# Attention and FP4 feed-forward block on one core: reciprocals as exp(-ln) on ScalarE, another order of loads and of the whole program, and 20 pairs of unread products

## The chip, the cores and the metric

The kernel runs on one NeuronCore of a Trainium2 chip. Its engines are TensorE (PE, matrix products into the PSUM banks), VectorE (DVE), ScalarE (ACT), GpSimdE (POOL) and SyncE (SP, which here only issues transfers). Each engine runs its own queue in order and waits on semaphores. The metric is the device time of one execution in microseconds, and the median of several executions is compared.

## The reference, cut to what matters

```python
x = L0_attn_x                                   # (8, 512, 128), float32
xn = (x - mean) / sqrt(var + 1e-5)
# attention branch, 16 heads of 8, two codes per head
q, k, v = heads(xn @ w_qkv.T)
q = q @ code.T * 8**-0.5;  k = k @ code.T * 8**-0.5      # two codes per head
q = softmax(q, axis=-1) * 8**-0.5
k_exp = exp(k - max(k, axis=rows))
kv = cumsum(k_exp * v, axis=rows) / (cumsum(k_exp, axis=rows) + 1e-9)
attn = sum(q * kv, over codes) @ w_out.T
# feed-forward branch, everything through block-wise FP4 (blocks of 16)
gate = fp4(xn) @ fp4(w_gate).T;  up = fp4(xn) @ fp4(w_up).T     # 352 wide
ffn = fp4(silu(gate) * up) @ fp4(w_down).T
out = x + attn + ffn
```

`fp4` divides a block of 16 by its largest magnitude over 6, rounds to the grid 0, 0.5, 1, 1.5, 2, 3, 4, 6 and multiplies back. The two denominators that matter for the change are the variance under the square root and, for every row, head and code, the product of the softmax sum of q and the running sum of k_exp.

## The kernel before, in words

The eight batches are the unit of the pipeline. One batch is a tile of 128 partitions by 512 elements (four rows of 128 on each partition). The program of each engine is a loop over steps with the pieces of work of several batches in it. Which batch a piece works on follows from `b = step - k`, and the order in which the pieces stand in the loop body is written out by hand (it differs on each engine). A piece that belongs to the weights or to the first batches stands under `if step == k`. So each engine has a fill (the weights are made FP4, the first batches enter), a part in which every step repeats the same pieces for other batches, and a drain.

In the repeated part one turn of TensorE is, by the names of the destinations: `t_ps` from `wv_t` (the values), `o_ps` (output rows), `t_ps` from `xq` (transposes), `h_ps` (transposes of the hidden blocks), `o_ps`, then the gate and up products `g_ps`, `u_ps`, the coded q and k products `a_ps` from `wqk_t` (called qk below), `t_ps` from `o_codes`, and so on to `a_ps` from `kv` and `before` (called the base product below: the column sums over the preceding rows).

The step that the change rewrites is the chain from the base product to `q_n`:

- ACT: `a_ps<-q_rel` (exp of the q codes), after the semaphore `base_done`
- DVE: `kv<-kv,a_ps` adds the base to the running sums (128x1152), `a_ps<-a_ps` adds the two exps, `den` multiplies both sums, in two instructions
- DVE: `den_r` is the reciprocal of `den`, and `q_n` is the exp times `den_r`
- POOL: `o_codes` is `kv` times `q_n`. TensorE waits for `qn_done` before the qk products of a later batch, since they write the same PSUM bank `a_ps`.

Beside it ACT brings `xq_t` from PSUM (TensorE waits for it before the gate product), makes the square `s_ps<-yx` of the rounding of x (DVE turns it into `sx` and `qx`) and the silus. Exp and Silu sit in different function tables, so ACT loads a table twice in a turn, and once more for the Sqrt of the variances of batches 2 to 7 (`sd`, line 551).

At the start TensorE multiplies `ident` by `before` 14 times (line 905) into `o_ps`, whose content nobody reads.

## Time and profile before

| | us |
|---|---|
| median of 3 executions | 153.87 (152.71 to 154.32) |
| the profiled execution | 152.51 |
| its span, first to last instruction | 150.8 |
| outside the span | 1.7 |
| first gate product of batch 0, 1, 2, 3 | 25.7, 40.2, 54.3, 68.7 |
| first gate product of batch 7 | 124.5 |

The profile is one execution. Its busy shares are means over a fill (to about 40 us), a repeated part (54.3 to 111.7 us, four turns of 14.33 us) and a drain (from 124.5 us), which have different limits. Each stretch is therefore read by itself. PE is TensorE's products, PEld its weight loads. "x2" behind a product of float32 numbers counts two records for one product.

### The profile page before, as it was taken

The numbers are of one execution on the slowest core, as the hardware profiler recorded it, in microseconds if no ns is written. First come the engines' busy times: TensorE is split into PE (matmuls) and PEld (weight loads), VectorE is DVE, ScalarE is ACT, GpSimd is POOL, SyncE is SP. The second block draws the span as 40 slices with busy tenths as digits, with TensorE's granted clock in tenths as the row PEclk, the third lists the DMA queues.
The fourth block names the chain that finished last, engine by engine and source line by source line (L and its number), as shares of the span: only waits on it lengthen the run. The fifth ranks groups of instructions, "written<-read, shape, count | busy, mean of one in ns | idle before, by whom it ended". The sixth has DMA issues, their size and how long they took to land.

```text
span 150.8 us, 2457 instructions
## 1 busy us (share of the span) xinstructions
PE 131.9 (87%) x817; PEld 106.2 (70%) x817; DVE 127.6 (85%) x326; ACT 111.4 (74%) x252; POOL 120.1 (80%) x123
## 2 busy tenths in 40 slices
PE   3937694998699999999999999999999999985591
PEld 3926373565476978797879778987988797675490
DVE  0699997169999999999999999999999989999601
ACT  0547549379889889988998899889894978592430
POOL 4418756616999999999999999999999999966710
PEclk9997555599999999999999999999999999999998
DMA  5980000000000001000100010001000100200101
GB/s 123 309 335 5 0 0 0 7 0 0 2 0 0 0 4 70 0 2 0 70 4 0 0 70 7 0 0 70 0 4 21 48 0 0 76 0 0 70 0 70
DMA packets 3932, 5.15 MB, mean 34 GB/s; under 512 B 528, under 2 KB 1872, under 8 KB 3920
## 3 DMA queue, kind: packets, MB, share of 16 engines
q1 hardware_dynamic: 2832, 4.36, 8.3%
q10 hardware_dynamic: 1088, 0.64, 1.5%
q8 instruction: 6, 0.10, 0.3%
q14 instruction: 6, 0.05, 0.1%
HBM read 2.90 MB, written 2.10 MB: 33 GB/s over the span
## 4 chain that ended last, share of the span: by engine, by line
PE 69%; DVE 11%; ACT 8%; DMA 4%; POOL 3%; ACTq 2%; issue 1%
PE t_ps L1040 5%; PE a_ps L928 4%; DMA x_all<-x 4%; PE g_ps L1073 4%; PE u_ps L1077 3%; PE u_ps L1074 3%; PE o_ps L1047 3%; PE o_ps L1012 3%; PE g_ps L911 3%; PE g_ps L935 3%; PE g_ps L974 3%; PE u_ps L953 3%; PE o_ps L918 3%; PE o_ps L1068 3%; PE t_ps L1003 3%; PE u_ps L984 2%
## 5 line engine op out<-in xcount | busy, mean ns | idle before, releaser
L349 POOL TENSOR_TENSOR kv<-v_sb,kv 128x512 f32<-128x512 f32 x16 | 16.9, 1075 | 0.0
L385 POOL TENSOR_TENSOR o_codes<-kv,q_n 128x1024 f32<-128x1024 f32 x8 | 15.8, 1972 | 1.4 <-DVE q_n L766 1.4
L438 POOL TENSOR_TENSOR yh<-h,h_r 128x704 f32<-128x704 f32 x8 | 11.1, 1385 | 5.7 <-ACT h_r L464 5.7
L608 ACT ACTIVATE xn<-x_all,shift,rstd 128x128 f32<-128x128 f32 x32 | 13.1, 481 | 1.4 <-POOL shift L433 1.4
L371 POOL TENSOR_TENSOR yh<-h,h_r 128x704 f32<-128x704 f32 x8 | 11.1, 1385 | 1.4 <-ACT h_r L557 1.4
L323 POOL TENSOR_TENSOR hq<-qh,h_max 128x704 f32<-128x704 bf16 x8 | 11.1, 1385 | 0.9 <-DVE qh L862 0.9
L342 POOL TENSOR_TENSOR yx<-xn,x_r 128x512 f32<-128x512 f32 x8 | 8.5, 1058 | 4.0 <-ACT x_r L504 4.0
L1040 PE MATMUL t_ps<-wv_t,xn_t 128*128 128x128 f32 x64 | 9.7, 299 | 2.1 <-ACT xn_t L494 1.9
L401 POOL TENSOR_TENSOR hq<-qh,h_max 128x704 f32<-128x704 bf16 x8 | 11.1, 1387 | 0.0
L1040 PEld LDWEIGHTS t_ps<-wv_t,xn_t 128*128 128x128 f32 x64 | 8.6, 208 | 3.2 <-ACT xn_t L494 3.2
L712 DVE TENSOR_TENSOR kv<-kv,a_ps 128x1152 f32<-128x1152 f32 x8 | 10.7, 1333 | 0.0
L569 ACT ACT_TABLE_LOAD x8 | 10.3, 1283 | 0.1
L928 PEld LDWEIGHTS a_ps<-wqk_t,xn_t 128*128 128x128 f32 x64 | 8.9, 211 | 1.8 <-ACT wqk_t L516 1.2
L928 PE MATMUL a_ps<-wqk_t,xn_t 128*128 128x64 f32 x64 | 9.0, 288 | 1.0 <-ACT wqk_t L516 1.0
L800 DVE TENSOR_TENSOR out_sb<-x_all,o_ps 128x512 f32<-128x512 f32 x8 | 5.4, 678 | 5.2 <-PE o_ps L918 5.2
L946 PE MATMUL t_ps<-ident,o_codes 128*128 128x128 f32 x32 | 7.5, 276 | 2.6 <-POOL o_codes L385 2.5
L477 ACT ACT_TABLE_LOAD x7 | 9.0, 1283 | 0.1
L334 POOL TENSOR_TENSOR xq<-qx,x_max 128x512 f32<-128x512 bf16 x8 | 8.5, 1057 | 0.6 <-DVE qx L751 0.6
L1073 PE MATMUL g_ps<-wg_t,xq_t 128*128 128x352 f32 x16 | 6.9, 519 | 2.2 <-ACT xq_t L562 2.2
L591 ACT ACTIVATE silu<-g_ps 128x352 f32<-128x352 f32 x8 | 3.7, 463 | 6.0 <-PE g_ps L911 6.0
L758 DVE RECIPROCAL den_r<-den 128x128 f32<-128x128 f32 x8 | 7.6, 944 | 0.1
L533 ACT ACTIVATE v_sb<-t_ps 128x512 f32<-128x512 f32 x8 | 4.8, 596 | 3.7 <-PE t_ps L1040 3.7
(195 smaller groups left out, 466.7 us busy)
## 6 DMA issues: line engine op xcount, KB each, us to landing
out<-out_sb SPq DMA_DIRECT2D x8, 256.0 KB, 2.0
x_all<-x SPq DMA_DIRECT2D x7, 256.0 KB, 6.2
x_all<-x ACTq DMA_DIRECT2D x1, 256.0 KB, 5.8
w_raw<-w_down SPq DMA_DIRECT2D x1, 176.0 KB, 4.5
wqk_raw<-w_qkv ACTq DMA_DIRECT2D x1, 128.0 KB, 3.5
w_raw<-w_gate SPq DMA_DIRECT2D x1, 128.0 KB, 3.1
w_raw<-w_up ACTq DMA_DIRECT2D x1, 128.0 KB, 3.9
wv_t<-w_qkv ACTq DMA_DIRECT2D x1, 64.0 KB, 5.5
```

Of the source, the lines that this page charges most:

```text
L323: nc.gpsimd.tensor_tensor(hq[:, 4 * p + 2:4 * p + 4, 0:FF].rearrange("p t (b k) -> p t b k", k=BLOCK), qh[:, p, 2 * FF:4 * FF].rearrange(" ...
L349: last = nc.gpsimd.tensor_tensor(heads(kv[:, p, :, c * D:(c + 1) * D]), heads(v_sb[:, p, :].rearrange("p (j d) -> p j d", j=TILES)), widen ...
L371: nc.gpsimd.tensor_tensor(blocks(yh[:, p, 2 * FF:4 * FF], PAIR * HB), h[:, p, 2 * HB:4 * HB, 0:BLOCK], spread(h_r[:, p, 2 * HB:4 * HB], PA ...
L385: nc.gpsimd.tensor_tensor(o_codes[:, p, :, :].rearrange("p j (c w) -> p j c w", w=HEAD), kv[:, p, :, 0:KV].rearrange("p j (c w) -> p j c w ...
L401: nc.gpsimd.tensor_tensor(hq[:, 4 * p + 0:4 * p + 2, 0:FF].rearrange("p t (b k) -> p t b k", k=BLOCK), qh[:, p, 0 * FF:2 * FF].rearrange(" ...
L438: nc.gpsimd.tensor_tensor(blocks(yh[:, p, 0 * FF:2 * FF], PAIR * HB), h[:, p, 0 * HB:2 * HB, 0:BLOCK], spread(h_r[:, p, 0 * HB:2 * HB], PA ...
L569: nc.scalar.activation(silu[:, 1, :], g_ps[:, 0:FF], ACT.Silu).then_inc(silu1_done, 1)
L608: last = nc.scalar.activation(xn[:, p, j * D:(j + 1) * D], x_all[:, b, j * D:(j + 1) * D], ACT.Identity, bias=shift[:, b, j:j + 1], scale= ...
L712: nc.vector.tensor_tensor(kv[:, p, :, :], kv[:, p, :, :], a_ps[:, 0:ROW].unsqueeze(1).broadcast_to([P, TILES, ROW]), ALU.add)
L928: last = nc.tensor.matmul(a_ps[:, 2 * j * HC:2 * (j + 1) * HC], xn_t[:, p, j * P:(j + 1) * P], wqk_t[:, :], start=(j == 0), stop=False, sk ...
L1040: last = nc.tensor.matmul(t_ps[:, j * P:(j + 1) * P], xn_t[:, p, j * P:(j + 1) * P], wv_t[:, :], start=True, stop=True)
L1073: nc.tensor.matmul(g_ps[:, 0:FF], xq_t[:, p, 1 * P:2 * P], wg_t[:, :], start=True, stop=True).then_inc(gate1_done, 1)
```

## The change

It rewrites three things and moves nearly all the rest.

1. `den_r` is no longer DVE's reciprocal. ACT computes `den_log = ln(den)` and `den_0 = exp(-den_log)`; DVE computes `den_p = den * den_0` and `den_r = (den_p - 2) * den_0`, which is a Newton step with the sign turned, and `q_n` takes the scale `-HEAD_SCALE`. The square root of the variances of batches 2 to 7 becomes `ln` and `exp(-0.5 * ...)` in the same way, in two groups (batches 2 and 3, batches 4 to 7). One table holds Exp and Ln, and is loaded by name.
2. The third piece of `w_up` goes to SP's queue, `w_down` to ACT's, and batch 1 of x to SP's.
3. Instead of 14 unread products there are 20 pairs, spread over the fill.

```diff
-            sp.dma_start(w_raw[:, 2 * FFP:], w_down).then_inc(down_in, 16)
-            for b in range(2, BATCHES):
+            sp.dma_start(w_raw[0:FF - 2 * P, FFP + 2 * P:2 * FFP], w_up[2 * P:FF, :]).then_inc(gu_in, 16)
+            for b in range(1, BATCHES):
...
-            act.dma_start(w_raw[0:FF - 2 * P, FFP + 2 * P:2 * FFP], w_up[2 * P:FF, :]).then_inc(gu_in, 16)
             act.dma_start(wv_t[:, :], w_qkv[2 * D:3 * D, :]).then_inc(wv_in, 16)
-            act.dma_start(x_all[:, 1, :], x_v[1]).then_inc(x_in[1], 16)
+            act.dma_start(w_raw[:, 2 * FFP:], w_down).then_inc(down_in, 16)
+            nc.scalar.preload_act_table_set(LOG_SET)
...
-                if step == 5:
-                    act.wait_ge(vareps2_done, 1)
-                    nc.scalar.activation(sd[:, 2:8, :], var_eps[:, 2:8, :], ACT.Sqrt).then_inc(sd2_done, 1)
+                if step == 6:
+                    act.wait_ge(vareps2_done, 1)
+                    nc.scalar.activation(var_log[:, 2:4, :], var_eps[:, 2:4, :], ACT.Ln).then_inc(vlog2_done, 1)
...
+                    act.wait_ge(den_done, b + 1)
+                    nc.scalar.activation(den_log[:, :, :], den[:, :, :], ACT.Ln).then_inc(dlog_done, 1)
...
+                    nc.scalar.activation(den_0[:, :, :], den_log[:, :, :], ACT.Exp, scale=-1.0).then_inc(dexp_done, 1)
...
+                    nc.vector.tensor_tensor(den_p[:, :, :], den[:, :, :], den_0[:, :, :], ALU.mult).then_inc(dprod_done, 1)
...
+                    nc.vector.scalar_tensor_tensor(out=den_r[:, :, :], in0=den_p[:, :, :], scalar=2.0, in1=den_0[:, :, :], op0=ALU.subtract, op1=ALU.mult).then_inc(denr_done, 1)
...
-                    nc.vector.reciprocal(den_r[:, :, :], den[:, :, :]).then_inc(denr_done, 1)
...
-            for _ in range(14):
-                nc.tensor.matmul(o_ps[:, 0:P], ident[:, :], before[:, :], start=True, stop=True)
...
+                if step == 7:
+                    for _ in range(2):
+                        nc.tensor.matmul(o_ps[:, 0:P], ident[:, :], before[:, :], start=True, stop=True)
```

The order of the pieces shows in the queues. ACT in a turn of the repeated part, from the copy of `xn_t` to the first silu, before:

```order
L494 ACTIVATE xn_t<-t_ps 128x512 [waits xnT_done]
L504 ACTIVATE x_r<-x_recip 128x32 [waits xrec_done]
L524 ACTIVATE a_ps<-q_rel 128x128 [waits base_done]
L528 ACTIVATE hq_t<-h_ps 128x384 [waits hqT2_done]
L533 ACTIVATE v_sb<-t_ps 128x512 [waits v_done]
L543 ACTIVATE s_ps<-yx 128x512 [waits qh0_done,yx_done]
L557 ACTIVATE h_r<-h_recip 128x44
L562 ACTIVATE xq_t<-t_ps 128x512 [waits xqT_done]
L569 ACT_TABLE_LOAD
L569 ACTIVATE silu<-g_ps 128x352 [waits gate1_done]
```

The same place of ACT now:

```order
L484 ACTIVATE a_ps<-q_rel 128x128 [waits base_done]
L489 ACTIVATE x_r<-x_recip 128x32 [waits xrec_done]
L505 ACTIVATE h_r<-h_recip 128x44 [waits hrec1_done]
L516 ACTIVATE s_ps<-yh 128x352 [waits yh0_done]
L521 ACTIVATE v_sb<-t_ps 128x512 [waits v_done]
L534 ACTIVATE hq_t<-h_ps 128x384
L538 ACTIVATE den_log<-den 128x128 [waits den_done]
L551 ACTIVATE den_0<-den_log 128x128 [waits dlog_done]
L556 ACTIVATE xq_t<-t_ps 128x512 [waits xqT_done]
L563 ACTIVATE s_ps<-yx 128x512 [waits qh0_done,yx_done]
L567 ACT_TABLE_LOAD
L567 ACTIVATE silu<-g_ps 128x352 [waits gate1_done]
```

The copy `xq_t` now stands behind both new functions, which wait for DVE's `den`, and the square `s_ps<-yx` stands behind `xq_t` instead of ahead of it. DVE at the same place of a turn, before:

```order
L640 RECIPROCAL x_recip<-x_max 128x32 [waits xmax_done]
L645 SCALAR_TENSOR_TENSOR sh<-s_ps,yh 128x352 [waits sqh0_done]
L661 RECIPROCAL h_recip<-h_max 128x44 [waits hmax1_done]
L679 SCALAR_TENSOR_TENSOR qh<-s_ps,sh 128x352 [waits sh0_done]
L712 TENSOR_TENSOR kv<-kv,a_ps 128x1152 [waits qexp_done]
L713 TENSOR_REDUCE a_ps<-a_ps 128x64
L723 SCALAR_TENSOR_TENSOR sx<-s_ps,yx 128x512 [waits sqx_done]
L729 SCALAR_TENSOR_TENSOR den<-kv,a_ps 128x4x16 [waits qsum_done]
L729 SCALAR_TENSOR_TENSOR den<-kv,a_ps 128x4x16
L751 SCALAR_TENSOR_TENSOR qx<-s_ps,sx 128x512 [waits sx_done]
L758 RECIPROCAL den_r<-den 128x128 [waits den_done]
L766 SCALAR_TENSOR_TENSOR q_n<-a_ps,den_r 128x128 [waits denr_done]
```

And now:

```order
L691 RECIPROCAL h_recip<-h_max 128x44 [waits hmax1_done]
L693 TENSOR_REDUCE a_ps<-a_ps 128x64 [waits qexp_done]
L695 TENSOR_TENSOR kv<-kv,a_ps 128x1152
L698 SCALAR_TENSOR_TENSOR den<-kv,a_ps 128x4x16 [waits badd_done]
L698 SCALAR_TENSOR_TENSOR den<-kv,a_ps 128x4x16
L703 SCALAR_TENSOR_TENSOR sh<-s_ps,yh 128x352 [waits sqh0_done]
L716 SCALAR_TENSOR_TENSOR qh<-s_ps,sh 128x352 [waits sh0_done]
L725 TENSOR_TENSOR den_p<-den,den_0 128x128 [waits dexp_done]
L766 SCALAR_TENSOR_TENSOR den_r<-den_p,den_0 128x128 [waits dprod_done]
L784 SCALAR_TENSOR_TENSOR sx<-s_ps,yx 128x512 [waits sqx_done]
L789 SCALAR_TENSOR_TENSOR q_n<-a_ps,den_r 128x128 [waits denr_done]
L802 SCALAR_TENSOR_TENSOR qx<-s_ps,sx 128x512 [waits sx_done]
```

`q_n` now stands behind `sx`, which waits for ACT's late square. TensorE at the end of the same turn, the products from the first gate product on, before:

```order
L1073 MATMUL g_ps<-wg_t,xq_t 128x352 [waits xqt_done]
L1074 MATMUL u_ps0<-wu_t,xq_t 128x352
L1077 MATMUL u_ps1<-wu_t,xq_t 128x352
L911 MATMUL g_ps<-wg_t,xq_t 128x352 [waits silu1_done]
L916 MATMUL o_ps<-wo_t,o_t 128x128 [waits hqt3_done]
L918 MATMUL o_ps<-wd_t,hq_t 128x128 x3
L928 MATMUL a_ps<-wqk_t,xn_t 128x64 [waits qn_done]
```

And now:

```order
L998 MATMUL g_ps<-wg_t,xq_t 128x352 [waits xqt_done]
L1001 MATMUL u_ps1<-wu_t,xq_t 128x352
L1015 MATMUL a_ps<-wqk_t,xn_t 128x64 [waits qn_done]
L1015 MATMUL a_ps<-wqk_t,xn_t 128x64 x3
L1022 MATMUL g_ps<-wg_t,xq_t 128x352 [waits silu1_done]
L1029 MATMUL u_ps0<-wu_t,xq_t 128x352
```

The qk products with their wait for `q_n` now come two products behind the gate product, where six stood between. At last TensorE's first instructions in the fill; before, 14 unread products, the weight product of line 968 and then the transposes of batch 0. Now:

```order
L1070 MATMUL o_ps<-before,ident 128x128 x2
L1098 MATMUL a_ps<-code_bd,wqk_raw 128x32 [waits codebd_done]
L1098 MATMUL a_ps<-code_bd,wqk_raw 128x32
L1119 MATMUL o_ps<-before,ident 128x128 x2
L1086 MATMUL o_ps<-before,ident 128x128 x2
L1103 MATMUL o_ps<-before,ident 128x128 x2
L1116 MATMUL o_ps<-before,ident 128x128 x2
L1122 MATMUL o_ps<-before,ident 128x128 x2
L1145 MATMUL t_ps<-ident,xn 128x128 [waits xn_done]
```

Eight pairs stand ahead of the weight product (the last is the first row here) and five behind it. One pair follows these transposes, three stand behind the first qk products and ahead of the transpose of `k_max`, and three more come one by one in the first two turns.

## Rows read from the trace of the kernel before

**Rows 1.** The page: the span, the busy times and the chain that ended last.

```profile
span 150.8 us, 2457 instructions
PE 131.9 (87%) x817; PEld 106.2 (70%) x817; DVE 127.6 (85%) x326; ACT 111.4 (74%) x252; POOL 120.1 (80%) x123
...
PE 69%; DVE 11%; ACT 8%; DMA 4%; POOL 3%; ACTq 2%; issue 1%
```

**Rows 2.** Stretches: length, busy PE, PEld, DVE, ACT, POOL, granted clock, DMA.

```profile
8.55:13.30 4.75, 1.81 (x12) 1.38 (x12) 4.55 (x21) 2.35 (x9) 2.63 (x3) 1.00 0.49 187
13.30:30.20 16.90, 13.20 (x41) 9.43 (x42) 12.67 (x62) 10.45 (x25) 11.18 (x15) 0.50 0.01 2
30.20:40.17 9.97, 8.01 (x42) 5.07 (x40) 8.55 (x20) 8.16 (x21) 5.45 (x5) 0.99 0.00 0
...
54.32:68.65 14.33, 14.33 (x98) 11.95 (x98) 13.85 (x31) 13.01 (x30) 14.06 (x13) 1.00 0.05 19
```

**Rows 3.** The fill in order of time: start, length, engine.

```profile
2.44 5.33 PE L905 MATMUL o_ps<-before,ident 128*128 128x128 f32 x28 [2.44 <-POOL head_of L365]
...
10.35 0.24 ACT L456 ACTIVATE w_r<-w_recip 128x48 f32<-128x48 f32 x1 [1.86 <-DVE w_recip L803]
```

**Rows 4.** The chain that ended last, in the fill and at the first turns.

```profile
16.31 0.90 PE h_ps L939 x3
17.21 0.23 PE t_ps L980
...
23.67 1.28 ACT L551
...
25.73 1.54 PE g_ps L1073 x2
...
29.61 1.06 PE g_ps L911 x2
...
40.17 0.86 PE g_ps L1073 x2
```

**Rows 5.** One turn in order of time, from q_n on.

```profile
98.36 0.29 DVE L766 SCALAR_TENSOR_TENSOR q_n<-a_ps,den_r 128x128 f32<-128x128 f32 x1
...
100.31 0.97 PEld L928 LDWEIGHTS a_ps<-wqk_t,xn_t 128*128 128x128 f32 x8
...
107.90 0.28 ACT L524 ACTIVATE a_ps<-q_rel 128x128 f32<-128x128 f32 x1
...
108.61 1.33 DVE L712 TENSOR_TENSOR kv<-kv,a_ps 128x1152 f32<-128x1152 f32 x1
...
109.12 0.60 ACT L533 ACTIVATE v_sb<-t_ps 128x512 f32<-128x512 f32 x1 [0.40 <-PE t_ps L1040]
109.62 0.60 ACT L543 ACTIVATE s_ps<-yx 128x512 f32<-128x512 bf16 x1
...
109.87 0.28 DVE L713 TENSOR_REDUCE a_ps<-a_ps 128x64 f32<-128x128 f32 x1
...
110.25 0.69 DVE L723 SCALAR_TENSOR_TENSOR sx<-s_ps,yx 128x512 f32<-128x512 f32 x1
...
110.47 0.60 ACT L562 ACTIVATE xq_t<-t_ps 128x512 f32<-128x512 f32 x1
...
110.86 0.34 DVE L729 SCALAR_TENSOR_TENSOR den<-kv,a_ps 128x64 f32<-128x64 f32 x2
...
111.72 0.94 DVE L758 RECIPROCAL den_r<-den 128x128 f32<-128x128 f32 x1
```

**Rows 6.** The chain that ended last, in the same turn: TensorE's slots.

```profile
100.58 0.84 PE a_ps L928 x8
...
107.38 0.49 PE a_ps L1019 x2
...
111.65 0.59 PE g_ps L1073 x2
```

**Rows 7.** The chain that ended last, in the drain.

```profile
136.94 0.96 DVE den_r L758
```

More of the change, by code:

```diff
@@ new lines, in _ @@
+                    dve.wait_ge(badd_done, b + 1)
+                    for c in range(CODE):
+                        last = nc.vector.scalar_tensor_tensor(out=den[:, :, c * HEADS:(c + 1) * HEADS], in0=kv[:, p, :, KV + c * HEADS:KV + (c + 1) * HEADS],
+                                                              scalar=DEN_EPS, in1=a_ps[:, ROW + TILES * HC:ROW + TILES * (HC + HEADS)].rearrange("p (j h) -> p j h", j=TILES),
+                                                              op0=ALU.add, op1=ALU.mult)
@@ new lines, in _ @@
+                if step == 5:
+                    dve.wait_ge(wsq_u_done, 1)
+                    nc.vector.scalar_tensor_tensor(out=w_s[:, FFP:2 * FFP], in0=u_ps[0][:, 0:FFP], scalar=OFFSET, in1=w_y[:, FFP:2 * FFP],
+                                                   op0=ALU.add, op1=ALU.subtract)
+                if step == 6:
+                    dve.wait_ge(x_in[5], 16)
+                    for j in range(TILES):
+                        last = nc.vector.bn_stats(stats[:, 5, j, :], x_all[:, 5, j * D:(j + 1) * D])
@@ new lines, in _ @@
+                if step == 10:
+                    for c in range(CHUNKS):
+                        last = nc.tensor.transpose(h_ps[:, c * P:(c + 1) * P], w_dq[:, 2 * FFP + c * P:2 * FFP + (c + 1) * P], ident[:, :])
+                if step == 3:
+                    for _ in range(2):
+                        nc.tensor.matmul(o_ps[:, 0:P], ident[:, :], before[:, :], start=True, stop=True)
+                b = step - 9
+                if 0 <= b < BATCHES:
+                    p = b % 2
+                    if b < BATCHES - 1:
+                        pe.wait_ge(vev_done, b + 2)
+                    if b == 0:
+                        pe.wait_ge(xq_done, b + 1)
+                    for j in range(TILES):
+                        last = nc.tensor.transpose(t_ps[:, j * P:(j + 1) * P], xq[:, p, j * P:(j + 1) * P], ident[:, :])
+                    last.then_inc(xqT_done, 1)
@@ new lines, in _ @@
+                b = step - 11
+                if 0 <= b < BATCHES:
+                    p = b % 2
+                    pe.wait_ge(hqt2_done, b + 1)
+                    for c in range(CHUNKS):
+                        last = nc.tensor.transpose(h_ps[:, c * P:(c + 1) * P], hq[:, 4 * p + 3, c * P:(c + 1) * P], ident[:, :])
+                    last.then_inc(hqT3_done, 1)
+                    nc.tensor.matmul(o_ps[:, 2 * P:3 * P], o_t[:, p, 2 * P:3 * P], wo_t[:, :], start=True, stop=False)
+                    for c in range(CHUNKS):
+                        last = nc.tensor.matmul(o_ps[:, 2 * P:3 * P], hq_t[:, 2, c * P:(c + 1) * P], wd_t[:, c * P:(c + 1) * P], start=False, stop=(c == CHUNKS - 1))
@@ L908, in _ @@
+                b = step - 9
                 if 0 <= b < BATCHES:
@@ L911, in _ @@
                     nc.tensor.matmul(g_ps[:, 0:FF], xq_t[:, p, 0 * P:1 * P], wg_t[:, :], start=True, stop=True).then_inc(gate0_done, 1)
-                b = step - 6
+                if step == 3:
+                    for _ in range(2):
+                        nc.tensor.matmul(o_ps[:, 0:P], ident[:, :], before[:, :], start=True, stop=True)
+                b = step - 9
+                if 0 <= b < BATCHES:
+                    p = b % 2
+                    nc.tensor.matmul(u_ps[0][:, 0:FF], xq_t[:, p, 0 * P:1 * P], wu_t[:, :], start=True, stop=True).then_inc(up0_done, 1)
+                b = step - 11
                 if 0 <= b < BATCHES:
```

1021 lines of the change are left out of this document (539 added, 482 removed).

## The prediction

> **What bounds the kernel now.** I read the page first [rows 1]: TensorE is busy 87% of a span of 150.8 us and has 69% of the chain that ended last, but DVE, POOL and ACT have 85, 80 and 74%, so every engine is nearly full and the order of the queues decides. Then the table of stretches [rows 2], because the means hide three different limits. In the repeated part a turn is 14.33 us and TensorE is busy for all of it, at a granted clock of 1.00 (2.4 GHz). There nothing that DVE, ACT or POOL gains shortens the time; an added wait of TensorE lengthens it. DVE has 13.85 us of work in such a turn, ACT 13.01, POOL 14.06, so 0.5, 1.3 and 0.3 us are free. In the fill the clock is 0.50 (1.2 GHz) from 13.3 to 30.2 us; it fell after a stretch from 8.55 to 13.30 in which TensorE was busy 1.81 of 4.75 us, and rose after an unbroken row of products. The first gate product of batch 0 takes 1.54 us, that of batch 1 0.86 [rows 4]. So the fill is the place where time is to be had, and the repeated part the place where it can be lost five times over. The sum is made against the profiled execution, 152.51 us (span 150.8 and 1.7 around it); that is 1.4 below the median of 153.87, and I carry the difference over to the median.
>
> **The loads.** The third piece of w_up has the same place in time on SP's queue as it had on ACT's, ahead of w_down instead of beside it, and batch 1 of x is issued some 0.5 us earlier. The reciprocal that waits for the weights' maxima still comes behind both, and `w_r` starts at 10.35 [rows 3]. What could be earlier by the loads is at most the half microsecond of the issue; I take 0, range -0.5 to +0.3. What hides them is DVE, busy 4.55 of 4.75 us there [rows 2].
>
> **The fill up to the first gate product of batch 0.** First the unread products. Fourteen took 5.33 us, 0.38 each [rows 3]. Now 26 of the 40 stand ahead of the transposes of batch 0: from 2.44 sixteen end at 8.5, the weight product takes 0.5, ten more end at 12.9. `xn` of batch 0 now stands behind `w_r` on ACT, hence starts at 10.5 and ends at about 12.2, so the products cost it 0.7 us. Transposes, copy, a pair (0.8), the value products and the qk products bring TensorE to about 16.2, and three more pairs (2.3 us) to 18.5, where the transpose of `k_max` stood at 17.2 [rows 4]. That is **+1.3 us**. From there to the gate product it took 8.5 us. Of the nine pieces of TensorE on the chain from 16.31 to 29.61 (the first and the last are shown), three lie between that transpose and the gate product, 3.9 us together at half clock [rows 4]. Since TensorE is busy almost without a gap from 2.4 to 18.5 now, I take it that the clock stays at 2.4 GHz in what follows, and every piece falls by 40 to 50%, as the gate product's 1.54 to 0.86: about **-1.8 us** on the pieces up to the gate product. The table load for Sqrt, 1.28 us on the chain [rows 4], and the square root behind it go, since Ln and Exp share the resident table; four small functions for batches 2 and 3 come in their place, at some 0.1 each behind other work: **-1.2 us**. Sum -1.7: the first gate product at 24.0 instead of 25.7. Two things could keep it later: w_q of the up weights is now rounded behind `qx` and `k_max`, about 4 us later, and the copy of the values of batch 1 stands behind a wait for the statistics of batches 2 and 3. Laid end to end both are ready within 0.5 us of that time, so they take the gain's place if it grows, and bound it: -2.5 at most. At the other end is 0, if the products that hold TensorE (1.3 and 0.7 us) are not repaid by the clock.
>
> The Trainium skill (ScalarE: Activation LUTs, section What ACT_TABLE_LOAD costs) puts a switch of sets at 1283 ns of load and some 1380 ns of drain. The load agrees with the row at 23.67; the drain doesn't show here, the next function starts 0.01 us behind the load in this chain. By that page the vanished load would be worth 2.66 us and the forecast 1.4 us lower; I keep the row.
>
> **From there to the first gate product of batch 1**, 14.44 us before. The three pieces up to 30.2 and the gate product lose about 2.2 us if the clock is full. Against it stand one pair (0.76) and, new in front of `xq_t`, the two functions of the denominators of batch 0: 0.28 each, as the exp of the same size [rows 5], less what DVE and ACT have free, +0.5. Sum **-1.0**, from -2 to 0. The next turn has one pair more; it had 0.7 us of waiting that the pair partly fills: **+0.2**. The group of batches 4 to 7 (ten small pieces on ACT, DVE and POOL) is in this stretch, and POOL is the fuller one of them; it is in the range.
>
> **The repeated part.** DVE loses a reciprocal of 0.94 us [rows 5] and gains two operations over 128 elements. None like it with both operands in SBUF is in the trace; the nearest are q_n (0.29, one operand in PSUM) and half of `den` (0.17), so 0.2 to 0.3 each, 0.5 together. ACT gains 2 x 0.28. Both engines keep room (13.4 and 13.6 of 14.33), so as sums they cost and give nothing. The order does. Before, q_n was done at 98.65 and the qk products that wait for it had their slot at 100.58 [rows 5, 6], 1.9 us of slack. Now the chain after the base product (which ends at 107.87 [rows 6]) runs: exp 107.90 to 108.18; reduction from 108.22; `kv` from 108.43 to 109.76; `den` to 110.14; ln 110.18 to 110.46; exp 110.50 to 110.78 (handovers of 0.04 as between the rows; an independent piece starts 0.07 to 0.1 before the one ahead ends, as 109.12 + 0.60 against 109.62) [rows 5]. Then `xq_t` 110.68 to 111.28. TensorE's gate product has its slot at 111.65 and its weight load some 0.27 earlier (100.31 against 100.58), so `xq_t` is just in time. The square now behind it runs 111.18 to 111.78 instead of ending at 110.22, `sx` starts at 111.82, and **q_n ends at 112.73**. The qk products stand only two products of 0.59 behind the gate product now: slot 112.83, weight load 112.56. It can start at 112.78. The wait is **0.2 us a turn**. What is late next is the first silu, behind the table load (111.78 to 113.06) at 113.5, for a gate product whose load comes at about 113.6: covered by 0.1. In the rest of the turn the order of TensorE is as it was, the queues behind have 0.2 to 0.6 us of room by the same walk (POOL's `hq` behind `qh` the least), and POOL's `o_codes` starts as before. Nothing gives the wait back. Over five turns, batch 2 to batch 7: **+1.0 us**. The ends: 0, if each of the nine handovers is 0.02 shorter, and +3, if ln and exp take 0.46 like a function of 352 elements or the gate product is late too.
>
> **The drain.** The reciprocal of the last batch, 0.96 us on the chain [rows 7], becomes ln, exp and two DVE operations, 1.2 us, but `sh` and `qh` of half a microsecond each now run beside them instead of ahead of `kv`, and the last table load comes 0.45 us earlier in ACT's queue. I take **-0.4**, from -0.9 to +0.4.
>
> Sum: -1.7 - 1.0 + 0.2 + 1.0 - 0.4 = **-1.9 us**. 153.87 - 1.9 = **152.0 us**, 1.2% faster.
>
> **The rivals.** *No wait in the repeated part, and the fill gives all.* The walk leaves 0.2 us, which the handovers can hide; the fill gives 2.5 and 1.5 and the drain 0.4, less 0.2: -4.2 and **149.7 us**. Against it: DVE and ACT are in a row of waits for each other in the fill, and each late piece shifts all behind it.
>
> *The clock falls again.* Behind the third pair at 18.5 TensorE has to wait for `k_negmax`, the weights' rounding and the copies, as in the stretch in which it fell before; but its busy share there, some two thirds by my walk, is nearer to the 8.01 of 9.97 us from 30.2 to 40.2, where the clock stayed, than to the 1.81 of 4.75 where it fell [rows 2]. If it falls at about 22 and rises at about 27, 1.8 to 2 us come back: -0.1 and **153.8 us**. The Trainium skill (TensorE: Matmul & The Clock Gate, section A second HAM failure mode) has a kernel in which short idle times between groups of products were enough for the clock to swing. By it this rival would be the likelier one, at 153.8; the stretch from 30 to 40 us, with short waits and a full clock, speaks against it here.
>
> *Slower: the denominator's chain becomes the bound.* All from the base product to q_n and `xq_t` is now one chain through three engines, 4.9 us long beside 4.96 us of products, with both new functions ahead of `xq_t`. If ln and exp together take 0.36 us more than I have (0.46 each), `xq_t` and q_n both come that much later, and with the silu behind the table load the wait is about 0.6 to 0.8 us a turn. It decides from 0.6 us a turn on, six turns with batch 1: 3.6 to 4.8 against the 3.1 of fill and drain. At 0.8: +1.9 and **155.8 us**. For it: the exact closeness of the two sums. Against: the exp of the same size takes 0.28 and its table holds both.
>
> **How the numbers follow.** The forecast's case 0.46, no wait and a full gain 0.18, the clock 0.17, slower 0.19. About 1% (1.5 us) is what a measurement of this kernel tells from no change. The case of the forecast runs from 151 to 153.2, and two thirds of it lie below 152.3; with the first rival that is 0.50 faster. The rest of it and most of the clock's case are 0.31 the same; slower 0.19. The range from 149.6 to 155.2 leaves out the outer parts of the first and the last rival, 2 in 10.
>
> **What the profile of the changed kernel would show.** The granted clock at 1.00 from 13 to 30 us; 17 table loads instead of 18; the first gate products (line 998) of batch 0 near 24.0, of batch 1 near 37.5; turns of 14.5 us with a wait of TensorE for q_n ahead of line 1015; DVE waiting ahead of `sx`; new functions of 0.28 us. I would be wrong if the turns are 14.33 or above 14.7, or if the clock is at 0.50 for more than 3 us behind the first products.

## The result, and the profile after

The changed kernel takes **158.02 us** (median of 4 runs, 157.31 to 158.48) against 153.31 us of the kernel before in the same comparison: a ratio of **1.030**, 95% interval 1.022 to 1.038. It is 3% slower, where 152.0 us had been predicted, and lies above the end of the range (155.2). A ratio in this document leaves out executions that were over 1.5% slower than the fastest of the same kernel; a median is over all of them. The profiled execution took 158.48 us. Its page, with the busy times, the granted clock and the chain by engine:

```profile
span 156.7 us, 2589 instructions
PE 135.6 (86%) x869; PEld 108.8 (69%) x869; DVE 135.0 (86%) x333; ACT 115.7 (74%) x274; POOL 121.2 (77%) x126
...
PEclk9999959999999999999999999999999999999999
...
PE 52%; DVE 28%; ACT 9%; DMA 4%; POOL 3%; issue 1%; SPq 1%
```

Beside [rows 1] the chain tells more than the busy times do. TensorE had 69% of it and has 52%; DVE now has 28%. DVE is busy 135.0 us where it was 127.6, though the reciprocal of the denominators is gone from it. The fill is shorter and the repeated part longer. The first gate product of batches 0, 1, 3 and 4, in TensorE's rows in order of time:

```profile
24.02 0.86 PE L998 MATMUL g_ps<-wg_t,xq_t 128*128 128x352 f32 x2 [0.69 <-ACT xq_t L556]
36.85 0.86 PE L998 MATMUL g_ps<-wg_t,xq_t 128*128 128x352 f32 x2 [1.17 <-ACT xq_t L556]
...
67.94 0.76 PE L998 MATMUL g_ps<-wg_t,xq_t 128*128 128x352 f32 x2
83.64 0.76 PE L998 MATMUL g_ps<-wg_t,xq_t 128*128 128x352 f32 x2
```

Batch 0 is at 24.0 where it was at 25.7, batch 1 at 36.9 where it was at 40.2 [rows 4]: 3.3 us gained. Then a turn takes 15.70 us (83.64 - 67.94) in place of 14.33, and everything is given back, with 5.9 us more of span in the end. The chain in one such turn, from the end of the base product (L1163) to the qk products (L1015):

```profile
63.83 0.50 PE a_ps L1163 x2
...
64.36 0.29 ACT a_ps L484
...
64.97 1.26 DVE kv L695
...
66.25 0.35 DVE den L698 x2
66.61 0.44 DVE sh L703
...
67.07 0.52 DVE qh L716
67.60 0.56 DVE den_p L725
...
68.18 1.36 DVE den_r L766
69.54 0.60 DVE sx L784
70.14 0.21 DVE q_n L789
...
70.39 1.10 PE a_ps L1015 x8
```

All of it is DVE from 64.67 on, and `den_r`, costed at 0.2 to 0.3 us, is its longest piece with 1.36. The two longest waits of the trace both end with `q_n` (us in total, times, longest):

```profile
PEld a_ps L1015 <- DVE q_n L789: 9.3, 6, 1.8
POOL o_codes L374 <- DVE q_n L789: 8.8, 8, 2.0
```

Why two operations over 128 elements take so long is to be seen where DVE and POOL stand side by side. DVE's rows of this turn, and then POOL's:

```profile
67.52 0.63 DVE L725 TENSOR_TENSOR den_p<-den 128x128 f32<-128x128 f32 x1
68.18 1.36 DVE L766 SCALAR_TENSOR_TENSOR den_r<-den_p,den 128x128 f32<-128x128 f32 x1
```

```profile
65.88 2.12 POOL L346 TENSOR_TENSOR kv<-v_sb,kv 128x512 f32<-128x512 f32 x2
67.95 1.44 POOL L353 TENSOR_TENSOR yh<-h,h_r 128x704 f32<-128x704 f32 x1
```

POOL's product ends at 68.00 and `den_p` at 68.15; POOL's `yh` ends at 69.39 and `den_r` at 69.54. Both DVE operations end 0.15 us after the POOL instruction that was running when they started, whatever their own length. In this trace that is so in all 13 cases in which one of them started beside a POOL instruction (0.14 to 0.15 us). In the last but one batch it is the other way round: `den_p` takes 1.02 us beside a POOL instruction that ends at 130.79, and `den_r` behind it, with POOL idle, takes 0.29. The groups of the two over the whole kernel (minimum, median, maximum in ns):

```profile
L725 DVE TENSOR_TENSOR den_p<-den x8: 279/626/1023, 36.5 to 143.2; 128x128 f32<-128x128 f32 x8
L766 DVE SCALAR_TENSOR_TENSOR den_r<-den_p,den x8: 291/1356/1358, 37.2 to 143.6; 128x128 f32<-128x128 f32 x8
```

That gave the theory to test: **a DVE operation that reads both operands from SBUF is held up until POOL's instruction ends** (theory A). The Trainium skill (SBUF — State Buffer, section Who interferes with whom) states it: such an instruction shares a read interface with a POOL instruction that reads SBUF, and the one that comes second is blocked for all of the other's duration. The times above agree, but for one thing: only 0.15 us are left to do when the POOL instruction has ended, where the operation takes 0.28 by itself. Every POOL instruction beside them here reads SBUF, so no run shows whether one that doesn't would hold them up too. The prediction had seen that no such operation was in the trace of before, and bounded the price by operations with one operand in PSUM. Theory B is that the order of the queues, with ln and exp inside the chain, makes the lateness; theory C that the operations are slow by their form.

### The profile page after: what moved, and what is told of

It is laid out like the page before. It is cut to its first block, busy times and chain, and to the rows that moved or that the text cites. A ratio compares the mean times of both kernels' runs of the same rounds, so it can differ in the third digit from the quotient of the medians.

```text
span 156.7 us, 2589 instructions
## 1 busy us (share of the span) xinstructions
PE 135.6 (86%) x869; PEld 108.8 (69%) x869; DVE 135.0 (86%) x333; ACT 115.7 (74%) x274; POOL 121.2 (77%) x126
## 4 chain that ended last, share of the span: by engine, by line
PE 52%; DVE 28%; ACT 9%; DMA 4%; POOL 3%; issue 1%; SPq 1%
DVE kv L695 6%; DVE den_r L766 5%; PE a_ps L1015 5%; DMA x_all<-x 4%; PE g_ps L1022 4%; PE g_ps L1045 3%; PE g_ps L1094 3%; PE u_ps L1067 3%; PE u_ps L1029 3%; PE o_ps L1036 3%; PE o_ps L1156 3%; DVE sx L784 3%; PE u_ps L1126 3%; PE a_ps L1163 2%; DVE den_p L725 2%; DVE qh L716 2%
## 5 line engine op out<-in xcount | busy, mean ns | idle before, releaser
L1015 PEld LDWEIGHTS a_ps<-wqk_t,xn_t 128*128 128x128 f32 x64 | 7.8, 191 | 9.5 <-DVE q_n L789 9.3
L1015 PE MATMUL a_ps<-wqk_t,xn_t 128*128 128x64 f32 x64 | 8.6, 278 | 6.3 <-DVE q_n L789 6.3
L353 POOL TENSOR_TENSOR yh<-h,h_r 128x704 f32<-128x704 f32 x8 | 11.4, 1422 | 0.0
L567 ACT ACT_TABLE_LOAD x8 | 10.3, 1283 | 0.1
L766 DVE SCALAR_TENSOR_TENSOR den_r<-den_p,den 128x128 f32<-128x128 f32 x8 | 8.7, 1090 | 0.3
L998 PE MATMUL g_ps<-wg_t,xq_t 128*128 128x352 f32 x16 | 6.4, 479 | 2.3 <-ACT xq_t L556 2.3
L1051 PE MATMUL t_ps<-ident,o_codes 128*128 128x128 f32 x32 | 7.5, 274 | 0.8 <-POOL o_codes L374 0.8
L575 ACT ACTIVATE s_ps<-yh 128x352 f32<-128x352 bf16 x8 | 3.7, 467 | 5.8 <-DVE qx L802 5.5
L1052 PE MATMUL t_ps<-ident,o_codes 128*128 128x128 f32 x32 | 7.4, 273 | 0.0
```

The lines of the kernel that those rows point to most:

```text
L353: nc.gpsimd.tensor_tensor(blocks(yh[:, p, 2 * FF:4 * FF], PAIR * HB), h[:, p, 2 * HB:4 * HB, 0:BLOCK], spread(h_r[:, p, 2 * HB:4 * HB], PA ...
L567: nc.scalar.activation(silu[:, 1, :], g_ps[:, 0:FF], ACT.Silu).then_inc(silu1_done, 1)
L766: nc.vector.scalar_tensor_tensor(out=den_r[:, :, :], in0=den_p[:, :, :], scalar=2.0, in1=den_0[:, :, :], op0=ALU.subtract, op1=ALU.mult).t ...
L1015: last = nc.tensor.matmul(a_ps[:, 2 * j * HC:2 * (j + 1) * HC], xn_t[:, p, j * P:(j + 1) * P], wqk_t[:, :], start=(j == 0), stop=False, sk ...
```

## Experiments

**1. The first guess in PSUM.** One operand of each of the two operations moves to a part of a PSUM tensor that is free at that time.

```diff
-nc.scalar.activation(den_0[:, :, :], den_log[:, :, :], ACT.Exp, scale=-1.0)
+nc.scalar.activation(a_ps[:, 0:TILES * HC]..., den_log[:, :, :], ACT.Exp, scale=-1.0)
-nc.vector.tensor_tensor(den_p[:, :, :], den[:, :, :], den_0[:, :, :], ALU.mult)
+nc.vector.tensor_tensor(den_p[:, :, :], den[:, :, :], a_ps[:, 0:TILES * HC]..., ALU.mult)
 # and the same for den_r
```

> The changed kernel, with one edit: the first guess exp(-ln) is written to a free part of the PSUM tensor of the base product, so that the two operations of the Newton step have one operand in SBUF and one in PSUM, where they had both in SBUF. Nothing else moves. Theory A (a DVE operation with both operands in SBUF is held up while POOL works): the product takes 0.28 to 0.35 us where it took 0.63 (median), the second operation 0.28 to 0.35 where it took 1.36; the 1.3 to 1.4 us come off each of the six turns and the time is 150 to 151.5 us. Theory B (the lengthened time is of the chain itself: ln and exp ahead of the transposing copy, q_n late for the qk products by the order): the two operations may be shorter, but something else is as late, the turns stay above 15.3 us and the time is 156.5 to 158.5. Theory C (the operation is slow by its form, two arithmetic steps on 128 elements, whatever its operands): both durations and the time stay as they are, 158.

**150.70 us** (149.69 to 151.39), ratio to before 0.989 (0.981 to 0.997). The groups of the two operations, and the chain by engine on its page:

```profile
L725 DVE TENSOR_TENSOR den_p<-den,a_ps x8: 277/277/278, 34.7 to 134.8; 128x128 f32<-128x128 f32 x8
L766 DVE SCALAR_TENSOR_TENSOR den_r<-den_p,a_ps x8: 286/288/288, 35.0 to 135.1; 128x128 f32<-128x128 f32 x8
...
PE 72%; ACT 10%; DVE 8%; POOL 3%; DMA 3%; issue 1%; SPq 1%
```

The same operations on the same numbers take 0.28 and 0.29 us in every batch, with POOL busy beside them as before. The turn is 14.58 us (first gate product at 63.97 and 78.54), 1.12 less, and where the guess is stored makes 7.3 us between the two medians (6.3 by the two ratios to before). Theory C falls, and of B no more is left in the repeated part than 0.25 us a turn.

**2. No Newton step.** Both operations are left out and `q_n` takes the first guess.

```diff
-nc.vector.tensor_tensor(den_p[:, :, :], den[:, :, :], den_0[:, :, :], ALU.mult)
-nc.vector.scalar_tensor_tensor(out=den_r[:, :, :], in0=den_p[:, :, :], scalar=2.0, in1=den_0[:, :, :], ...)
-nc.vector.scalar_tensor_tensor(out=q_n..., scalar=-HEAD_SCALE, in1=den_r[:, :, :], ...)
+nc.vector.scalar_tensor_tensor(out=q_n..., scalar=HEAD_SCALE, in1=den_0[:, :, :], ...)
```

> The changed kernel without the Newton step: both DVE operations are left out and q_n takes the first guess exp(-ln) itself (this part of the computation is left out, and the reciprocals are the less exact for it). Theory A (the two operations are what costs, since POOL holds them up): turns of 14.3 to 14.5 us, q_n ends about 0.6 us earlier than with the step at full speed, the time is 149.7 to 151 us. It should be at most 0.5 us faster than the kernel with the guess in PSUM, as the two operations at 0.28 are little. Theory B (order and ln/exp): 156 to 158 us, since both functions and their place remain.

**150.51 us**, ratio 0.986 (0.980 to 0.992), turns of 14.58: no different from experiment 1. So the two operations cost nothing that can be measured once they aren't held up, and the 0.25 us a turn above 14.33 are not theirs.

**3. The reciprocal back, in the new order.** The headline of the change undone, all the rest kept.

```diff
-nc.scalar.activation(den_log[:, :, :], den[:, :, :], ACT.Ln)
-nc.scalar.activation(den_0[:, :, :], den_log[:, :, :], ACT.Exp, scale=-1.0)
-nc.vector.tensor_tensor(den_p[:, :, :], den[:, :, :], den_0[:, :, :], ALU.mult)
+nc.vector.reciprocal(den_r[:, :, :], den[:, :, :])
```

> The changed kernel with the denominators' reciprocal back on DVE in place of ln, exp and the two operations of the Newton step; it stands where the product of the step stood. The new order, the loads, the unread products and the variances' exp(-ln) stay. So it is the change without its headline part. The DVE reciprocal has one operand; it took 0.94 us before. Theory A: the operation isn't held up (0.9 to 1.0 us), and the repeated part has turns of 14.4 to 14.7; time 150 to 152 us. Theory B (the new order itself makes q_n late, whatever computes the reciprocal): turns above 15.3 and 156 us or more. If it is faster than the kernel with the guess in PSUM, the new way of computing has no gain in the repeated part at all.

**150.23 us**, ratio 0.984 (0.978 to 0.989). The reciprocal takes 0.94 us in every batch: it has one operand and isn't held up. The turns are 14.58 again. What the whole change has of gain is in the fill (first gate product of batch 1 at 34.7 us for 40.2), since every later turn is longer than before; the new way to compute the denominators' reciprocal brings nothing even where it isn't held up.

**4. POOL's instruction moved away from `den_r`.** `o_codes`, which waits for `q_n`, stands ahead of `yh` on POOL, so POOL is idle while `den_r` runs.

```diff
+                    pool.wait_ge(qn_done, b + 1)
+                    nc.gpsimd.tensor_tensor(o_codes[:, p, :, :]...)   # from behind yh
                     ... yh (L353)
```

> The changed kernel with one move on POOL: the scaling of the code columns by q_n (o_codes) stands ahead of the rounding step of the hidden half (yh, 1.4 us) that ran beside den_r. DVE's own queue is as it was. Theory A: POOL now waits for q_n where den_r runs, so den_r takes 0.29 us in place of 1.36, while den_p, still beside POOL's kv product, stays at 0.6; q_n is about 1.0 us earlier. The turns fall from 15.7 to 14.7 to 15.2, if the later yh doesn't take the place of the wait; time 151.5 to 155. The duration of den_r is the test here, more than the time. Theory C (slow by its form): den_r stays at 1.36.

**161.11 us**, ratio 1.058 (1.051 to 1.065). The two operations:

```profile
L725 DVE TENSOR_TENSOR den_p<-den x8: 281/730/814, 34.6 to 141.3; 128x128 f32<-128x128 f32 x8
L766 DVE SCALAR_TENSOR_TENSOR den_r<-den_p,den x8: 291/292/293, 35.2 to 141.6; 128x128 f32<-128x128 f32 x8
```

DVE's instructions are word for word those of the changed kernel; only what POOL does beside them changed, and `den_r` falls from 1.36 to 0.29 us. That is the test, and A holds. My time of 151.5 to 155 was wrong, though. POOL now waits 12.4 us in all for `q_n`, `yh` comes after that, ScalarE's square waits for it (10.3 us in all), and DVE for the square. This ring of POOL, ScalarE and DVE is the chain in the repeated part: its turns of 15.4 us are only 0.3 shorter than the 15.7 of the changed kernel, though `den_r` gave back 1.07. What makes the kernel slower than the changed one is the drain: from the last first gate product to the end it takes 30.6 us in place of 26.5, with the same ring behind the last batches (in this execution the clock also fell to 0.81 in the last 8.5 us).

**5 and 6. The denominators alone, in the order of before.** Ln and exp stand on ScalarE behind the copy of `xq_t`, the Newton step in the place of DVE's reciprocal, once with all operands in SBUF and once with the guess in PSUM.

```diff
                     nc.scalar.activation(xq_t[:, p, :], t_ps[:, :], ACT.Copy)
+                    nc.scalar.activation(den_log[:, :, :], den[:, :, :], ACT.Ln)
+                    nc.scalar.activation(den_0[:, :, :], den_log[:, :, :], ACT.Exp, scale=-1.0)   # or a_ps
-                    nc.vector.reciprocal(den_r[:, :, :], den[:, :, :])
+                    (den_p and den_r as in the changed kernel)
```

> The kernel before with the denominators alone changed: ln and exp stand on ScalarE behind the copy of xq_t, the two operations of the Newton step stand in the place of DVE's reciprocal, all operands in SBUF. Order, loads, variances and unread products are those of before. Theory A (POOL holds such an operation up until its own instruction ends): the product ends 0.15 us after POOL's yh (98.12 in the trace of before), the second operation 0.15 us after the POOL product behind it (98.9), so they take 0.7 to 0.9 us each and q_n ends near 99.3 to 99.4 in place of 98.65. The qk products have their slot at 100.58, so this order hides it; what is left is 0.5 us of lateness on POOL (o_codes) and DVE, and the table load on ScalarE 0.6 us later. Turns of 14.4 to 15.0 us, time 153 to 156. Theory C (the loss in the changed kernel is of the order alone): the two operations take 0.28 each here and the turns are as in the sister kernel with the guess in PSUM.

> The same kernel (before with the denominators alone changed), with the first guess in a free part of the PSUM tensor of the base product. Theory A: both operations take 0.28 us, q_n ends near 98.2 to 98.4; the difference to the sister kernel with all operands in SBUF is the hold-up alone, 0.3 to 0.6 us a turn, 2 to 4 us in all. Turns of 14.33 to 14.5, time 152 to 154: no gain over before, since TensorE was busy for all of the turn.

**181.32 and 181.94 us**, ratios 1.18 (1.16 to 1.20) and 1.19 (1.17 to 1.20). Both expectations failed, by something that I had overlooked. ScalarE in a turn of the first of them (the trace names the first guess `den`):

```profile
109.31 1.28 ACT L572 ACT_TABLE_LOAD   x1
110.61 0.31 ACT L572 ACTIVATE den_log<-den 128x128 f32<-128x128 f32 x1
110.94 1.28 ACT L574 ACT_TABLE_LOAD   x1
112.23 0.31 ACT L574 ACTIVATE den<-den_log 128x128 f32<-128x128 f32 x1
112.56 1.28 ACT L581 ACT_TABLE_LOAD   x1
```

Ln and exp each loaded a table of their own, since these kernels don't name the set that holds both, as the changed kernel does (`preload_act_table_set(LOG_SET)`): four loads a turn in place of two, a turn of 17.5 us. The Trainium skill (ScalarE: Activation LUTs, section Table sets: the hidden batching unit) counts one load for ln and then exp, because one set has both; here that holds only where the set is loaded by name. Of the hold-up these two tell one thing: DVE came so late that POOL had run dry, and the operations with both operands in SBUF took 0.29 us.

**7 and 8. The same with the set loaded by name.**

```diff
+                    nc.scalar.preload_act_table_set(LOG_SET)
                     act.wait_ge(kshift_done, b + 1)
                     nc.scalar.activation(kv[:, p, :, KV:ROW]..., ACT.Exp)
```

> The kernel before with the denominators alone changed, all operands in SBUF, as in the run in which two more table loads a turn hid everything; now the table that holds both ln and exp is loaded by its name ahead of the exp of the keys, so that ln and exp need no load of their own. Two table loads a turn, as before. Theory A (POOL holds an operation with two SBUF operands up): ln and exp end near 97.5 on the time scale of the trace of before, POOL's yh runs until 98.1 and its next product until 98.9; so the first operation takes 0.6 to 0.8 us and the second 0.7 to 0.8, q_n ends near 99.3 instead of 98.65, which the slot of the qk products at 100.58 hides, but POOL's o_codes starts 0.4 us later. The silu behind the table load comes 0.7 us later (98.7 for 98.04). Turns of 14.5 to 15.2, time 153.5 to 157. Theory C (nothing of the kind in this order): both at 0.29.

> The same kernel with the named table, and with the first guess in PSUM. Theory A: 0.28 us each for both operations, q_n at 98.4, o_codes on time. What is left of the change in this order is ScalarE's: the first silu is 0.6 to 0.7 us later, and the gate product that waits for it has its slot 0.3 to 0.5 us behind it now. So turns of 14.33 to 14.8, time 152.5 to 155, faster than with all operands in SBUF by 0 to 3 us. If it is as slow as with SBUF, the hold-up costs nothing in this order, and the order of the changed kernel is what made it costly.

**159.35 us** with SBUF, ratio 1.043 (1.036 to 1.050), and **158.97 us** with PSUM, ratio 1.044 (1.035 to 1.052). The groups of the first, and then of the second:

```profile
L775 DVE TENSOR_TENSOR den_p<-den x8: 293/744/769, 40.6 to 143.0; 128x128 f32<-128x128 f32 x8
L777 DVE SCALAR_TENSOR_TENSOR den_r<-den_p,den x8: 291/766/770, 41.4 to 143.3; 128x128 f32<-128x128 f32 x8
```

```profile
L775 DVE TENSOR_TENSOR den_p<-den,a_ps x8: 286/289/290, 39.1 to 141.4; 128x128 f32<-128x128 f32 x8
L777 DVE SCALAR_TENSOR_TENSOR den_r<-den_p,a_ps x8: 286/288/289, 39.4 to 141.7; 128x128 f32<-128x128 f32 x8
```

The durations came as expected from POOL's ends (0.6 to 0.8 and 0.7 to 0.8 us), in another order of another kernel. The times did not: both are slower than I had written, and alike, with turns of 15.06 and 15.02. The chain by engine is the same on both pages; below it stand a row of DVE in the first of the two, and the same wait in the list of waits of the second (us in total, times, longest):

```profile
DVE 52%; ACT 20%; PE 14%; issue 4%; DMA 3%; POOL 2%; ACTq 1%
...
102.31 0.53 DVE L788 SCALAR_TENSOR_TENSOR sh<-s_ps,yh 128x352 f32<-128x352 f32 x1 [0.26 <-ACT s_ps L594]
...
DVE sh L788 <- ACT s_ps L594: 8.4, 7, 1.2
```

TensorE is off the chain. In a turn it runs from DVE's `den` over ScalarE's ln, exp, table load, silu and square back to DVE's `sh`; the gate product of tile 0 also waits for that silu (6.7 and 6.5 us in all). The Newton step and `q_n` run while DVE would wait for the square anyway. The hold-up of 0.9 us is real, but it only takes that wait from 1.2 us down to 0.26, and costs nothing. In this place the new way is some 6 us slower than the reciprocal with either placing of the guess, so by the delay on ScalarE and not by the hold-up.

**9. What the later unread products do.** Experiment 1 with 9 of the 20 pairs; the 11 later ones are left out.

```diff
-                if step == 7:   # and all of steps 8, 9 and 10
-                    for _ in range(2):
-                        nc.tensor.matmul(o_ps[:, 0:P], ident[:, :], before[:, :], start=True, stop=True)
```

> The changed kernel with the guess in PSUM and with 9 of the 20 pairs of unread products: the 9 first ones stay (they end near 8 us, as the 14 products of before), the 11 later ones are left out. Theory A1 (the later pairs hold the clock): TensorE has the small share of work that it had before between 9 and 13 us, the granted clock falls to 0.50 near 13 to 14 us and comes back after a long row of products, near 27 to 30. The pieces between take about double, so the first gate product comes at 23.5 to 25 us in place of 22.2 although 2.9 us of unread products are gone from the queue; the time is 1 to 2.5 us above that of the kernel with 20 pairs, 151.5 to 153. Theory B1 (the later pairs only cost time): the first gate product at 21.5 or earlier, and 148.5 to 150.

**153.19 us**, ratio 0.998 (0.993 to 1.002), by the ratios 1.3 us above experiment 1 (0.989) and 1.8 above experiments 2 and 3 (0.986 and 0.984), and no faster than before. The table of stretches (length, busy time of PE, PEld, DVE, ACT and POOL, granted clock), first with 9 pairs, then with 20:

```profile
8.55:13.30 4.75, 1.58 (x11) 1.16 (x11) 4.57 (x24) 3.57 (x13) 2.67 (x3) 1.00 0.53 201
13.30:22.00 8.70, 7.05 (x32) 5.95 (x31) 7.99 (x30) 5.34 (x16) 5.40 (x6) 0.52 0.00 1
```

```profile
8.55:13.30 4.75, 4.38 (x37) 4.00 (x37) 4.54 (x23) 3.96 (x13) 3.04 (x4) 1.00 0.49 187
13.30:22.00 8.70, 6.59 (x50) 5.31 (x48) 8.43 (x32) 6.66 (x19) 6.33 (x7) 1.00 0.01 3
```

With TensorE at 1.58 of 4.75 us of work the granted clock falls to 0.50 (1.2 GHz) behind it, as before the change [rows 2]; with 4.38 it stays at 1.00 (2.4 GHz). The busy time of this one stretch doesn't settle it in between: with 3.34 us the clock fell at 20 us in the changed kernel, with 3.08 it stayed in experiment 10. The first gate product is at 25.04 with fewer products and at 22.22 with more. Up to batch 1 experiment 1 is 5.1 us ahead of the kernel before (35.05 for 40.17). The later pairs, by the clock, account for 2.8 of it; 2.3 are there without them (37.88), and the longer turns behind it take 2.4 back, so nothing is left of these in the time. In both kernels the chain to the first gate product has no table load, where it had the 1.28 us of the Sqrt's; and with 9 pairs the clock is back at about 24 us, before the change at 30. Neither was tested alone. (This profiled execution took 154.52 us; in it the clock also fell in the drain, from the last first gate product to the end 28.2 us for 26.5 in experiment 1, so its span isn't to be compared.)

**10. `q_n` ahead of `sx`.** What is left of the turn, 14.58 against 14.33? In experiment 1 the weight load of the qk products waits 0.54 us for `q_n`, and `q_n` stands behind `sx`.

```diff
+nc.vector.scalar_tensor_tensor(out=q_n...)        # moved up
 nc.vector.scalar_tensor_tensor(out=sx[:, p, :]...)
-nc.vector.scalar_tensor_tensor(out=q_n...)
```

> The changed kernel with the guess in PSUM, and with q_n moved ahead of sx on DVE. In the kernel with the guess in PSUM DVE's sx waits for the square on ScalarE, and q_n stands behind it though all that it reads is there 0.6 us earlier; the weight load of the qk products waits 0.54 us for it and 0.25 us of that reach the turn (14.58 against 14.33). If this wait is all that is left of the loss in the repeated part, the turns are 14.33 to 14.4 here and the time falls by 1.0 to 1.3 us, to 149 to 149.7. Rival: sx and qx come 0.3 us later and a later wait (the silu's or the code columns') takes the place: turns of 14.5 to 14.6 and no gain.

**151.10 us**, ratio 0.983 (0.978 to 0.988), turns of 14.54. The wait for `q_n` is gone and the rival is right. ScalarE's and then the weight loads' rows:

```profile
79.37 1.28 ACT L567 ACT_TABLE_LOAD   x1
80.67 0.46 ACT L567 ACTIVATE silu<-g_ps 128x352 f32<-128x352 f32 x1
```

```profile
79.89 1.16 PEld L1015 LDWEIGHTS a_ps<-wqk_t,xn_t 128*128 128x128 f32 x8
81.18 0.30 PEld L1022 LDWEIGHTS g_ps<-wg_t,xq_t 128*128 128x128 f32 x2
```

The silu ends at 81.13 and the load of the gate product that waits for it starts 0.05 later. The first gate product started at 78.99, and the next one starts 2.19 behind it; two products of 0.59 to 0.60 and the qk products' 0.84 would give 2.03. The product itself then takes 0.86 us, where the first one took 0.76.

**11. The reciprocal back, and `q_n` ahead of `sx`.** Experiments 3 and 10 together.

```diff
 (experiment 3, and)
+nc.vector.scalar_tensor_tensor(out=q_n...)        # moved up
 nc.vector.scalar_tensor_tensor(out=sx[:, p, :]...)
-nc.vector.scalar_tensor_tensor(out=q_n...)
```

> The changed kernel with the reciprocal back on DVE (no ln, exp and Newton step for the denominators) and with q_n ahead of sx. With the guess in PSUM and q_n ahead of sx, the wait moved from the qk products to the gate product that waits for the first silu behind the table load (turns of 14.54): ln and exp stand ahead of that load on ScalarE. Without them the silu comes 0.5 us earlier and both waits should be gone: turns of 14.33 to 14.4 us, time 148.5 to 149.8. Rival: the reciprocal's 0.94 us makes q_n or qx late and the turns stay at 14.5 to 14.6; time 150 to 151.

Ratio 0.993 (0.988 to 0.997), median 151.73 us, with one of 12 executions at 467.57 us, for which I have no cause. The median of the seven executions behind the ratio is 151.32 us. The turns are 14.54 once more: even without ln and exp the silu starts 1.68 us behind the first gate product, exactly as in experiment 10. So ln and exp are not what makes the silu late in the new order; my expectation failed. What ScalarE gained it waits away: its square, which stands ahead of the table load, now waits 0.18 us for DVE's `qh` (L708). In both kernels `qh` ends 0.34 us before the first gate product starts and the square starts 0.24 before it. What follows the square is the same in both: table load, silu, with the gate product only three pieces of TensorE later.

**12. The up product ahead of the gate product.** Experiment 10 and one swap on TensorE.

```diff
+nc.tensor.matmul(u_ps[0][:, 0:FF], xq_t[:, p, 0 * P:1 * P], wu_t[:, :], ...)
 pe.wait_ge(silu1_done, b + 1)
 nc.tensor.matmul(g_ps[:, 0:FF], xq_t[:, p, 0 * P:1 * P], wg_t[:, :], ...)
-nc.tensor.matmul(u_ps[0][:, 0:FF], xq_t[:, p, 0 * P:1 * P], wu_t[:, :], ...)
```

> The changed kernel with the guess in PSUM, q_n ahead of sx, and on TensorE the up product of tile 0 ahead of the gate product of tile 0 (both stood there in the other order). In the kernel without this swap the turn is 14.54 us: the gate product's weight load starts 0.05 us after the first silu ends, which is 0.2 us later than the products ahead of it allow. The up product (0.59 us) doesn't need the silu and covers that. If the silu is the last wait left in the repeated part, turns are 14.33 to 14.36 us there, and the time falls by 0.9 to 1.1 us, to 149.5 to 150.2. Rival: the gate product is now 0.4 us later than before the swap, so the second silu and what stands behind it on ScalarE are that much later, another product waits for them, and the turns stay at 14.5 to 14.8; time 151 or more.

**150.47 us** (150.01 to 151.37), ratio 0.983 (0.978 to 0.988), turns of 14.45. The wait for the silu is gone, and half of the gain is lost again elsewhere: the two products on `k_negmax` (L1137) start 0.52 us behind the group ahead of them, where it is 0.42 in experiment 1. Their weight load waits up to 0.3 us for DVE's `k_negmax` in three turns of this trace and not at all in the same turns of experiment 1. Why DVE brings it later wasn't tested. The time is in the middle between what I had expected and the rival. Of the kernels that compute the whole reference, this one, experiment 10 and experiment 3 are about equal, some 1.7% faster than before and 4 to 5% faster than the changed kernel.

## Why the prediction was wrong

**The step that failed** is the price of the two new DVE operations: "0.2 to 0.3 each, 0.5 together". They took 0.63 and 1.36 us (medians) on the chain. The premise stood beside it: none like them with both operands in SBUF was in the trace. They were bounded from the nearest rows, and those had an operand in PSUM, which is just the thing that matters (experiments 1, 4, 7 and 8). The bound was missing at the upper end: the rows for it were those of POOL, 0.80 to 1.97 us long and almost without gaps (14.06 of 14.33 us). With what was measured `q_n` comes 1.4 us later than in my walk, and the forecast changes sign. Of it 1.12 us reach each turn (15.70 against 14.58), six times, which is 6.7 of the 7.3 us. The prediction's own sign of being wrong, turns above 14.7, has come.

**The fill.** Without the hold-up it was better than forecast. The first gate product was foretold at 24.0 and is at 24.02 in the changed kernel, but in part by chance: in this execution the clock fell to 0.50 from 20 to 23 us, and in experiments 1 and 3, where it didn't, the product is at 22.2 to 22.3. So the gain of 1.7 us was half of the 3.5 that there are with a full clock, and the bound of 2.5 at most, from the rounding of w_q and the wait for the statistics, didn't hold. From there to batch 1 it was -1.6 (forecast -1.0). That the clock is 2.8 us of these gains is shown by experiment 9; the -1.2 us for the table load fits the chain, which no longer has it, and no run tested it alone. The rival in which the clock falls again came true in single executions, for 3 us, and is worth some 0.8 to 1.8 us (the first gate product at 23.00 in experiment 2, 24.02 in the changed kernel), where 1.8 to 2 had been given for five.

**The repeated part.** Turns of 14.5 with a wait for `q_n` of 0.2: experiment 1, which is the kernel as I had imagined it, has 14.58 with a wait that costs 0.25. The silu behind the table load, "covered by 0.1", was not: it is 0.2 late (experiments 10 and 11), and takes the wait's place when `q_n` is early. The last of the five turns was wrongly priced: 14.08 in experiment 1 for 13.03 before, +1.05 in place of +0.2. There the chain leaves TensorE and runs over `den`, ln, exp and `xq_t`, and half a microsecond of it goes with the new functions (13.55 in experiment 3). So the five turns cost 2.05 us where 1.0 was forecast.

**The drain.** From the last first gate product to the end it takes 26.5 us in place of 26.3, not 0.4 less. In sum experiment 1 is 2.0 us faster than before (by the medians) and I had said 1.9. That is luck: a fill that was better by 2.4 us and turns and a drain that were worse by 1.8, all mis-sized, nearly cancel in it.

**The rival on the other side** named the right chain and the right wait (TensorE for `q_n`), at 155.8 us, and the wrong link. Ln and exp were to be 0.46 us each; they took 0.31 or less. It had 0.19 of the chance.

**The loads** were forecast at 0. No run undid them alone, so this stays open.

## What to carry to other kernels

Before an operation moves to DVE in a kernel in which POOL is busy, look where its operands are: with both in SBUF its price here was its own length of 0.29 us, or the rest of the POOL instruction beside it and 0.15, whichever was longer, so 0.36 to 1.36; and with one in PSUM it was its own length. When a new operation is bounded by rows of a trace, the row has to share the thing that the operation contends for, not only the shape; if there is none such, the other engine's instruction length is the upper end. And a faster way to compute something off the bound is worth its risk only if an experiment without it is slower: experiment 3 was as fast with the old reciprocal.

## What the runs showed of the hardware

A held-up operation ends 0.14 to 0.16 us after the POOL instruction that ran when it started (68.00 and 68.15, 69.39 and 69.54), in all 33 cases of the changed kernel and of experiments 4 and 7. POOL's next instruction, which starts in between, doesn't hold it up further and is itself a little longer: 1.42 us in the mean for `yh` (L353) in place of 1.38. The same operations with one operand in PSUM took 0.28 to 0.29 us in all batches of experiments 1 and 8, and DVE's reciprocal, with one operand, 0.94 us in experiment 3, POOL being busy beside them.

Where the set with both wasn't named, ln, exp and the silu behind them each loaded a table, 1.28 us each, four loads a turn in place of two. The same kernel takes 181 us so and 159 us with the set loaded by name.

The first gate product came between 22.06 and 24.02 us in single executions of the eight kernels that have all 20 pairs and the new order. In two of them the clock fell for about 3 us (23.00 and 24.02); in the other six it didn't, and they lie between 22.06 and 22.73. So a single trace of a fill is good to a microsecond, while the turns of 14.58 agree to 0.02 in four kernels. The time goes with it: experiment 1 took 149.69 and 150.03 us at a mean granted clock of 1.00, and 151.36 and 151.39 at 0.99.
